# Cross attention of a two-layer model: keys turned by DMA, normalisation ahead of the reciprocal, routing of the last three groups in closer steps

## What is computed

```python
def _L1_xattn_ref(image_embeds, latents, ...):   # image_embeds = ctx, latents = layernorm(x)
    x = layer_norm(image_embeds, ln1_g, ln1_b)
    l = layer_norm(latents, ln2_g, ln2_b)
    q = l @ Wq                                    # 16 heads of 64
    kv = jnp.concatenate([x, l], axis=1) @ Wkv    # 64 + 64 rows a sequence
    ...                                           # softmax(q k^T / 8) v, then @ Wo
x = x + _L0_xattn_ref(...)
x = x + _L0_ffn_ref(...)
x = x + _L1_xattn_ref(ctx_1024, _layernorm(x), ...)
x = x + _L1_ffn_ref(_layernorm(x), ...)           # 8 experts, the best 2 of each token
```

## Time and profile before

| | |
|---|---|
| median of 3 runs | 1599.52 us (1598.59 to 1602.85) |
| the profiled execution | 1598.53 us |
| its span, first to last instruction | 1596.6 us |
| PE, busy time and share of the span | 1392.2 us, 87% |
| DVE | 1355.3 us, 85% |
| ACT | 1280.3 us, 80% |
| POOL | 1079.0 us, 68% |
| cross attention and routing | from some 395 us to 1311 us of the span |

### The profile page before, as it was taken

The page is one execution under the profiler, slowest core; times in us unless marked ns, Lnnn a source line. Parts: engine busy times, 40 slices in busy tenths (PEclk is TensorE's granted clock), DMA queues, the critical chain, the costliest instruction groups (busy, mean ns, idle before and its releaser), DMA issues. The chain is left out here.

```text
span 1596.6 us, 53031 instructions
## 1 busy us (share of the span) xinstructions
PE 1392.2 (87%) x17084; PEld 1186.1 (74%) x17084; DVE 1355.3 (85%) x3979; ACT 1280.3 (80%) x3930; POOL 1079.0 (68%) x1524
## 2 busy tenths in 40 slices
PE   4779889974799999999999999999999719999970
PEld 3667777763688888888888888888888618888860
DVE  4479999995799999999999999999999628888877
ACT  1358888875799999999999999999999616666645
POOL 0367877763666577887788778877887555666650
PEclk7989999986899999999999999999999959999995
DMA  5445553400100000000000000000000013332209
GB/s 145 140 158 180 192 202 148 160 2 5 27 13 12 13 20 20 23 22 19 18 22 22 18 18 22 22 18 18 22 15 9 22 43 91 87 84 77 80 28 316
DMA packets 99738, 101.83 MB, mean 64 GB/s; under 512 B 15305, under 2 KB 81132, under 8 KB 99457
## 3 DMA queue, kind: packets, MB, share of 16 engines
q1 hardware_dynamic: 82496, 78.77, 15.4%
q0 software_dynamic: 8640, 16.93, 3.2%
q10 hardware_dynamic: 8448, 4.20, 0.9%
HBM read 39.40 MB, written 57.16 MB: 60 GB/s over the span
## 5 line engine op out<-in xcount | busy, mean ns | idle before, releaser
L1227 ACT ACTIVATE c_p<-bank,c_nmax 128x128 f32<-128x128 f32 x1024 | 368.9, 401 | 2.2 <-DVE c_nmax L1081 1.3
L1016 POOL TENSOR_TENSOR c_p<-c_p,c_rden 128x512 f32<-128x512 f32 x256 | 266.8, 1042 | 110.4 <-DVE c_rden L1091 106.0
L1227 ACT ACTIVATION_READ_ACCUMULATOR c_p<-bank,c_nmax 128x1 f32 x1024 | 244.2, 241 | 0.0
L1403 POOL DMA_INDIRECT moe_outputs<-e_y,e_to x142 | 152.9, 1077 | 93.3 <-DVE e_y L1434 58.6
L112 PE MATMUL bank<-c_kvT,qk_fused 128*128 128x128 f16 x1024 | 185.8, 220 | 10.8 <-ACT c_kvT L1206 10.4
L1081 DVE TENSOR_REDUCE c_nmax<-bank 128x4 f32<-128x512 f32 x256 | 173.4, 677 | 17.5 <-PE bank L114 14.3
L114 PE MATMUL bank<-c_kvT,qk_fused 128*128 128x128 f16 x1024 | 185.7, 220 | 0.0
L113 PE MATMUL bank<-c_kvT,qk_fused 128*128 128x128 f16 x1024 | 185.7, 220 | 0.0
L1473 ACT ACTIVATE e_h<-bank,moe_b 128x256 f32<-128x256 f32 x284 | 117.9, 466 | 65.7 <-PE bank L114 64.4
L1297 PE MATMUL bank<-const,c_p 128*128 128x128 f32 x1024 | 155.9, 275 | 3.6 <-DVE c_pT0rest L1102 1.7
L1059 POOL DMA_INDIRECT moe_slots<-r_rows,r_pos x128 | 131.6, 1028 | 34.9 <-issue 34.9
(11 more groups left out here) (324 smaller groups left out, 5921.0 us busy)
## 6 DMA issues: line engine op xcount, KB each, us to landing
moe_slots<-slot_fill SPq DMA_DIRECT2D x66, 520.0 KB, 5.6
e_rows<-moe_slots SPq DMA_DIRECT2D x71, 130.0 KB, 2.2
f_z<-moe_outputs SPq DMA_DIRECT2D x32, 256.0 KB, 4.9
x<-in_x SPq DMA_DIRECT2D x16, 256.0 KB, 3.2
a_ctx<-in_ctx SPq DMA_DIRECT2D x32, 128.0 KB, 3.4
moe_stage<-in_L_ffn_W SPq DMA_DIRECT2D x16, 256.0 KB, 3.1
c_rows<-in_ctx SPq DMA_DIRECT2D x128, 32.0 KB, 2.0
c_rows<-x SPq DMA_DIRECT2D x128, 32.0 KB, 1.8
```

Of the source, the lines that this page charges most:

```text
L1016: pool.tensor_tensor(pr[r % 4][:], pr[r % 4][:], rep(rden[r % 4][:], 2, P), ALU.mult).then_inc(m["pn"], 1)
L1227: last = act.activation(pr[r % 4][:, h, :], SB[r % 2][:, P * h:P * h + P], ACT.Exp, bias=nmax[r % 4][:, h:h + 1], accum_out=den[r % 4][:, ...
L1403: pool.indirect_dma_start(s.z, bass.IndirectOffsetOnAxis(ap=to[t % YBUF][:, h:h + 1], axis=0), ys[t % YBUF][:, h, :], None, bounds_check=2 ...
```

## The change

- Keys: SP turns a tile's four f16 blocks with one transposing DMA, from `kvs` to `kvt`, which now has four buffers and a semaphore for each; TensorE's four transposes, ACT's copy and the waits that kept them apart from routing's use of the bank KVR go. G waits for the DMA. The row loads are made for two tiles at a time, four DMAs of 64 KB, two buffers.
- DVE: the normalisation of a tile's rows (`AT_KVN`) stands behind the row maximum and ahead of the reciprocal; before it stood at the end of the step, behind the statistics.
- Routing: the offsets of groups 0 to 12 are four steps smaller. Groups 13 to 15 have offsets of their own, with one step between an item and the next, and each of them has its own `rows`, `pf`, `pos` and scatter semaphore, so nothing waits for the landing of the scatters of the group before. The walk ends at step 282, not 299.

```diff
-        kvt = [sb(f"c_kvT{n}", [P, 2, 4, 64], F16) for n in range(2)]
+        kvt = [sb(f"c_kvT{n}", [P, 2, 4, 64], F16) for n in range(4)]
-        rows = sb("r_rows", [P, GT, ROW], F16)
+        rows = [sb(f"r_rows{n}", [P, GT, ROW], F16) for n in range(4)]
...
-        ROUTE_STATS = 14
-        ROUTE_RSTD, ROUTE_XN, ROUTE_XT, ROUTE_LOGITS, ROUTE_TOP, ROUTE_INDEX, ROUTE_MASK = 27, 32, 34, 38, 39, 42, 43
-        ROUTE_HIGH, ROUTE_LOW, ROUTE_STEP, ROUTE_BASE, ROUTE_POS = 44, 47, 45, 46, 47
+        EVEN = GROUPS - 3
+        ROUTE_STATS = 10
+        ROUTE_RSTD, ROUTE_XN, ROUTE_XT, ROUTE_LOGITS = (23, 23, 23), (28, 28, 24), (30, 29, 25), (34, 30, 26)
+        ROUTE_TOP, ROUTE_INDEX, ROUTE_MASK = (35, 31, 27), (38, 32, 28), (39, 32, 28)
+        ROUTE_HIGH, ROUTE_LOW, ROUTE_STEP = (40, 29, 25), (43, 30, 26), (41, 33, 29)
+        ROUTE_BASE, ROUTE_POS = (42, 33, 29), (43, 34, 30)
-        ROUTE_SCATTER = (48, 50, 51, 52, 54, 55, 56, 58)
-        FIRST, LO, HI, LAST = -15, 64, 240, CHUNKS + 43
+        ROUTE_SCATTER = tuple(zip((44, 46, 47, 48, 50, 51, 52, 54), (39, 40, 42, 43, 44, 46, 47, 48), (33, 34, 35, 36, 38, 39, 40, 41)))
+        FIRST, LO, HI, LAST = -15, 64, 224, CHUNKS + 26
...
+            if known(i):
+                for g in range(GROUPS):
+                    if 16 * i + k == 16 * g + at[min(max(g - EVEN + 1, 0), 2)]:
+                        return g
                 return None
+            return None if (k - at[0]) % 16 else i + (k - at[0]) // 16
+
+        def own(g):
+            return max(g - EVEN + 1, 0) if known(g) else 0
...
+            def load(n):
+                if n >= 2:
+                    sp.wait_ge(m["kvn"], 2 * n - 2)
+                for half in range(2):
+                    rows = slice(64 * half, 64 * half + 64)
+                    to = cs[n % 2]
+                    sp.dma_start(to[rows, :, 1 - half, :], cvw[1 - half, 2 * n:2 * n + 2, :, :].rearrange("t s d -> s t d")).then_inc(c_loaded[n % 2], 16)
+                    sp.dma_start(to[rows, :, half, :], s.xg(n // 2)[rows, 2 * (n % 2):2 * (n % 2) + 2, :]).then_inc(c_loaded[n % 2], 16)
+
+            def turn_keys(v):
+                sp.wait_ge(m["kv"], v + 1)
+                if v >= 4:
+                    sp.wait_ge(m["s"], 4 * (v - 3))
+                sp.dma_start_transpose(kvt[v % 4][:].rearrange("p n a c -> p (n a c)").rearrange("p (b c) -> p b c", b=4),
+                                       kvs[v % 4][:].rearrange("p n b d -> p (n b d)")).then_inc(kvt_in[v % 4], 16)
+
+            load(0)
+            load(1)
+            for v in range(TILES):
+                turn_keys(v)
+                if v % 2 == 1 and v + 3 < TILES:
+                    load((v + 3) // 2)
...
+                if t := tile(i, k, AT_KVN):
+                    v, r, g = t
+                    a, b = mv[r % 2], rst[r % 2]
+                    dve.wait_ge(m["rstd"], v + 1)
+                    wait(dve, m["kv"], v - 3)
+                    for n in range(2):
+                        last = dve.tensor_scalar(kv[r][:, n, :], cs[r // 2][:, r % 2, n, :], a[:, n, 0:1], b[:, n:n + 1], ALU.subtract, ALU.mult)
+                    last.then_inc(m["kvn"], 1)
...
-                if t := tile(i, k, AT_KVT):
-                    v, r, _ = t
-                    act.wait_ge(m["kvt"], v + 1)
-                    wait(act, m["s"], 4 * (v - 1))
-                    act.activation(kvt[r % 2][:].rearrange("p n a c -> p (n a c)"), KVB[:, 0:512], ACT.Copy).then_inc(m["kvt_copied"], 1)
...
                 if (g := group(i, k, ROUTE_HIGH)) is not None:
-                    wait(act, scattered, 128 * g)
-                    act.activation(rows[:, :, 0:D], r_xn[:], ACT.Copy).then_inc(mr["row_high"], 1)
+                    if own(g) == 0:
+                        wait(act, scattered[0], 128 * g)
+                    act.activation(rows[own(g)][:, :, 0:D], r_xn[:], ACT.Copy).then_inc(mr["row_high"], 1)
...
-                if t := tile(i, k, AT_KVT):
-                    pe.wait_ge(m["kv"], v + 1)
-                    wait(pe, m["kvt_copied"], v)
-                    for part in range(2):
-                        for b in range(2):
-                            at = 2 * P * part + P * b
-                            last = pe.transpose(KVB[:, at:at + P], kvs[r][:, part, b, :], s.ident_h[:])
-                    last.then_inc(m["kvt"], 1)
                 if n := number(i, k, AT_G, CHUNKS):
-                    if r % 4 == 0:
-                        pe.wait_ge(m["kvt_copied"], 4 * i + (k + AT_G) // 4 + 1)
+                    if u := tile(i, k, AT_G):
+                        pe.wait_ge(kvt_in[u[1]], 16 * (u[2] + 1))
```

More of the change, by code:

```diff
@@ L903, in cross_attention @@
     sem = s.sem
-    c_loaded = [sem(f"c_ctx_loaded{n}") for n in range(4)]
-    names = ("stats rstd kvn kv kvt kvt_copied g g_high g_copied s max exp rden pn pt pt_high pt_copied o o_high o_copied w x3")
+    c_loaded = [sem(f"c_ctx_loaded{n}") for n in range(2)]
+    kvt_in = [sem(f"c_kvt_in{n}") for n in range(4)]
+    names = ("stats rstd kvn kv g g_high g_copied s max exp rden pn pt pt_high pt_copied o o_high o_copied w x3")
     m = {n: sem("c_" + n) for n in names.split()}
@@ L908, in cross_attention @@
     mr = {n: sem("r_" + n) for n in route_names.split()}
-    scattered = sem("r_scattered")
+    scattered = [sem(f"r_scattered{n}") for n in range(4)]
     CHUNKS = 4 * TILES
@@ L944, in cross_attention @@
         pk = sb("r_pick", [P, 2, GT, EXPERTS])
-        pf = sb("r_posf", [P, 2, GT])
-        pos = sb("r_pos", [P, 2, GT], U32)
+        pf = [sb(f"r_posf{n}", [P, 2, GT]) for n in range(4)]
+        pos = [sb(f"r_pos{n}", [P, 2, GT], U32) for n in range(4)]
         zero = sb("r_zero", [P, 2, GT])
@@ L955, in cross_attention @@
         tx = sb("r_tx", [P, 72])
-        dest, first_choice = (rows[:, :, 2 * D + at:2 * D + at + 2].bitcast(F32) for at in (0, 2))
+        dest, first_choice = ([part[:, :, 2 * D + at:2 * D + at + 2].bitcast(F32) for part in rows] for at in (0, 2))
         block = ctx.enter_context(nc.Block())
@@ L959, in cross_attention @@
         PT, OB, KVR, WB = s.pb[4:8]
-        KVB = KVR[:].bitcast(F16)
         LOGITS = RANKS = KVR[:, 0:GT * EXPERTS]
@@ L999, in _ @@
         def _(sp):
-            def step(i, k):
-                t = 4 * i + k
-                if not (known(i) and i == 0):
-                    sp.wait_ge(m["kvn"], t - 3)
+            def load(n):
+                if n >= 2:
+                    sp.wait_ge(m["kvn"], 2 * n - 2)
                 for half in range(2):
                     rows = slice(64 * half, 64 * half + 64)
-                    sp.dma_start(cs[k][rows, 1 - half, :], cvw[1 - half, t, :, :]).then_inc(c_loaded[k], 16)
-                    sp.dma_start(cs[k][rows, half, :], s.xg(i)[rows, k, :]).then_inc(c_loaded[k], 16)
-            walk(sp, 0, TILES, 4, 4, TILES, step)
+                    to = cs[n % 2]
[13 more added lines that the diff above has]
+                    load((v + 3) // 2)
         @block.gpsimd
@@ L1068, in _ @@
             walk(pool, FIRST, LAST, 16, LO, HI, step)
-            pool.wait_ge(scattered, 128 * GROUPS)
+            pool.wait_ge(scattered[0], 128 * EVEN)
+            for q in range(1, 4):
+                pool.wait_ge(scattered[q], 128)
         @block.vector
@@ L1116, in step @@
                     dve.bn_aggr(mv[r % 2][:, 1, :], bst[:, 1, :]).then_inc(m["stats"], 1)
-                if t := tile(i, k, AT_KVN):
-                    v, r, g = t
-                    a, b = mv[r % 2], rst[r % 2]
-                    dve.wait_ge(m["rstd"], v + 1)
-                    wait(dve, m["kv"], v - 3)
-                    for n in range(2):
-                        last = dve.tensor_scalar(kv[r][:, n, :], cs[r][:, n, :], a[:, n, 0:1], b[:, n:n + 1], ALU.subtract, ALU.mult)
-                    last.then_inc(m["kvn"], 1)
                 if t := tile(i, k, -ROUTE_STATS):
                     v, r, g = t
+                    if not tile(i, k - 1, AT_STATS):
+                        dve.drain()
                     dve.bn_stats(r_bn[:, r, :], s.xg(g)[:, r, :])
@@ L1283, in step @@
                     v, r = n
-                    half, b, t = r % 2, r // 2 % 2, r // 4 % 2
+                    half, b, t = r % 2, r // 2 % 2, r // 4
                     pe.wait_ge(m["g_copied"], v + 2 if r % 4 == 0 else v - r % 4 + 4)
@@ L1288, in step @@
                         at = 8 * half + 2 * h
-                        last = parts_product(pe, SB[r % 2][:, P * h:P * h + P], [part[:, b, at:at + 2, :] for part in gs[t]],
+                        last = parts_product(pe, SB[r % 2][:, P * h:P * h + P], [part[:, b, at:at + 2, :] for part in gs[t % 2]],
                                              [kvt[t][:, part, 2 * b:2 * b + 2, :] for part in range(2)])
@@ L1316, in step @@
                     pe.wait_ge(mr["xn"], g + 1)
-                    wait_rows(i, k)
-                    wait(pe, mr["base_read"], g - 1 if ROUTE_XT + 16 < ROUTE_POS else g)
```

(1 more changed line is left out.)

52 lines of the change are left out of this document (21 added, 31 removed).

## The result

The changed kernel took 1595.45 us (median of 10 runs, 1590.74 to 1597.03) against 1600.38 us (10 runs) of the kernel before on the same chip: ratio 0.9969, 95% interval 0.9957 to 0.998. It is 5 us faster, and not 27.5: the time is 4 us above the upper end of the range, 1591 us, which is also that of rival (a). The profiled execution took 1595.94 us for a span of 1594.1 us.

The account below looks back on a forecast made before the run. The prediction took TensorE to bound the attention. Keys 28.1, start -3.5, order -9.1 and tail +12.0 made 27.5 us less: 1599.5 - 27.5 = 1572 us (forecast 1562 to 1580, chance 0.52; range 1553 to 1591).

Parts of the forecast that it names:

- rival (a): Attention: engines behind TensorE swallow the keys' gain, attention gains 0 to 10 us, time 1581 to 1591 us; chance 0.23.
- ACT was what was late there: Attention: TensorE's wait for ACT's copy of the turned keys goes without a next wait replacing it; 14.0 us kept.
- the 14.1 us of the turns: Attention: removing four key turns from TensorE saves 0.22 us a tile over 64 tiles, 14.1 us.
- the two terms: Attention: key turns off TensorE, 14.1 us, and the wait for the keys' copy gone, 14.0 us; sum 28.1 us.
- The term of the copy: Attention: waits for ACT's copy of the turned keys, 10.4 + 4.6 = 15.0 us, of which 14.0 us counted as gain.
- the bound of the stretch without routing: Attention's 16 chunks without routing: TensorE never waits and its work, 50.6 us, makes up the 50.5 us measured.
- Keys, forecast 24.6 us less with the start: Attention: keys by DMA gain 28.1 us, less 3.5 us at the start.
- Start, forecast 3.5: First tile: nothing covers the turned transfer before the first G product; cost 3.5 us, bounds 1 and 7.
- Transfer, forecast 4 us and hidden: Each tile's turned 128 KB DMA: 2.6 to 6.2 us, taken as 4, hidden inside about 7 us in steady state.
- Order, forecast a loss of 9.1: DVE's normalisation ahead of the reciprocal delays p rest: loss of 0.7 us in each of 13 groups, 9.1 us.
- Tail, forecast 12.0: Routing behind the attention: the last group's first scatter starts at 1285.5, 12.0 us sooner than 1297.57; bounds 10 and 13.

Follow-up runs that it names:

- e18: The kernel before with the keys' transfer alone (normalisation at the end of VectorE's step, rstd at offset 13, routing as before): 1602.75 us, ratio 1.0014.
- e17: The kernel before, unchanged, as a control: 1600.7 us, ratio 1.0001.
- e3: The kernel before with only the normalisation moved ahead of the reciprocal; keys turned by TensorE, routing as before: 1601.3 us, ratio 1.0006.
- e4: The changed kernel with the routing's offsets of before and one row buffer for every group: 1596.91 us, ratio 0.9976.
- e2: The changed kernel with GpSimd's rstd of the keys' rows one step sooner (offset 14, not 13): 1586.91 us, ratio 0.9917.
- e13: The changed kernel with rstd at offset 14 and the rest part of the heads' outputs for one head of eight only: 1642.59 us, ratio 0.9839.
- e9: The kernel before with the normalisation ahead of the reciprocal and rstd at offset 14; keys turned by TensorE, routing as before: 1696.62 us, ratio 1.0109.
- e15: The changed kernel with rstd at offset 14, same as e2, repeated as a control on another chip: 1668.18 us, ratio 0.9973.
- e10: The changed kernel with rstd at offset 14 and the routing's offsets and single row buffer of before: 1675.43 us, ratio 1.0003.
- e1: The changed kernel with the normalisation of the keys' rows behind the statistics again, at the end of VectorE's step: 1597.58 us, ratio 0.9979.

## Why the prediction was wrong

**Which step failed.** "ACT was what was late there, and it gets to its next copy, of p, about half a microsecond sooner than now, so I keep all: 14.0 us", and with it the 14.1 us of the turns. TensorE did run into the next wait. With the keys' transfer alone (e18 against e17, on one chip) the two terms, 28.1 us by the forecast less 3.5 for the start, brought nothing: 1602.75 against 1600.7 us, and a pace 0.34 us a group higher. That the turns went is seen chunk by chunk. The table shows, for each step of a group, the time from the start of TensorE's turn of p to the start of the next one (medians of nine groups, us, from the starts of those matmuls):

```
step              0    1    2    3    4    5    6    7    8    9   10   11   12   13   14   15    sum
before (e17)   3.32 3.93 3.58 3.10 3.32 3.10 3.96 3.10 3.32 3.10 3.10 3.18 3.47 3.28 3.44 3.25  53.57
order (e3)     3.63 3.63 3.58 3.10 3.52 3.25 3.96 3.10 3.32 3.10 3.10 3.10 3.50 3.25 3.23 3.10  53.47
keys (e18)     3.10 3.66 3.69 3.10 3.10 3.52 4.04 3.10 3.10 3.10 3.17 3.63 3.25 3.75 3.44 3.25  54.01
keys+order(e4) 3.62 3.25 3.58 3.10 3.76 3.25 3.96 3.10 3.10 3.10 3.10 3.14 3.73 3.25 3.23 3.10  53.36
after          3.61 3.25 3.96 3.10 3.10 3.18 3.10 3.18 3.83 3.25 3.23 3.10 3.73 3.25 3.54 3.10  53.54
rstd 14 (e2)   3.10 3.25 3.96 3.10 3.10 3.10 3.10 3.22 4.05 3.25 3.22 3.10 3.91 3.25 3.55 3.10  53.37
```

From before to keys alone each of steps 0, 4, 8 and 12 loses 0.22 us, the turns, 0.88 us in all, as forecast. Step 1 loses another 0.27: of the 0.66 us that TensorE waited there for the copy, the rest is lost to the next wait in the same step, now for the rest of G. Steps 5, 11 and 13 then give back 0.42, 0.45 and 0.47, steps 2 and 6 0.2: VectorE is now what is late. The term of the copy was also too large by its own rows: 10.4 + 4.6 us counts the six waits twice that stand under PE and under PEld alike. Each counted once, the 17 waits come to 11.9 us, 2.3 of them at the first three tiles.

That the bound has changed engine is seen by following the waits back from TensorE's matmul at 1100 us to 620 us, at each instruction to what released it, or else to the one before it on its engine (share of the 480 us):

```
                        PE   DVE   ACT  POOL
before (e17)            73    13    14     0
order alone (e3)        79     5    14     2
keys alone (e18)        41    46    13     0
after                   17    52     0    31
rstd sooner (e2)        37    62     0     0
lighter VectorE (e13)   68    21    10     0
```

The shares say which engine holds the chain, not how long a group is: in e9, with a pace of 54.98, TensorE has 54 and VectorE 46. Even before, a quarter of the chain did not run through TensorE. The prediction took the bound of the stretch without routing, where TensorE never waits, for that of the middle, where VectorE has 4 us more work a group. In e2 the chain of each group is one piece of 32.9 us on VectorE, its instructions back to back, and one of 20.5 us on TensorE. The kernel lets TensorE run only one chunk ahead of p rest, since the turned p has one bank; that this is why neither engine fills the other's thin chunks is argued, not shown.

**Term by term.** Keys, forecast 24.6 us less with the start: alone +2 us (0 to 4, e18); on top of the new order -5 (e3 to e4), none of it in the pace; with rstd sooner -18 to -19 from the pace (e9 against e15 and e10), because e9 is slow and not because e10 is fast. Start, forecast 3.5: first load to first G product is 1.6 us longer. Transfer, forecast 4 us and hidden: 2.9 us from the start of the issue, which takes 1.2 of them, hidden in every tile but the first. (The landings in the rows include the issue too, so the 0.6 us that the prediction added for it was counted twice; it changes nothing.) The estimate from the Trainium skill ("VectorE: DVE Perf Modes", The three transpose paths), 1309 ns a block and so 5.2 us for four, was too dear here. The same page's preference for TensorE (Rules for kernel authors), which the prediction set aside, came out right for the keys' transfer alone.

Order, forecast a loss of 9.1: nothing alone (e3), and with the keys' transfer a gain of 6 us (e18 to e4, 1.0014 to 0.9976). The wait for rstd was foreseen and real (8.8 us in 400), but it hid the other half: at its old place the pair costs more, 0.64 us an instruction (e1) against 0.42. The Trainium skill ("SBUF — State Buffer", Who interferes with whom), with its lock between VectorE's fast modes and GpSimd, pointed the right way: by that rule alone the move would only gain, and the instructions of the pair did become shorter in e3 too (0.37 against 0.52 us in e17), though there the time didn't.

Tail, forecast 12.0: 10.3. POOL had more left than I counted: five of group 14's eight scatters stand before rstd and hold it up until 2.3 us behind the statistics, three more stand behind it. What I had not priced is that the same scatters, laid closer under groups 13 to 15, slow these: 5.2 us in groups 14 and 15, and 7 us in the whole stretch, against e4. Net the routing gave 1 us in the changed kernel and 5.6 us with the pair at its old place (e18 to e1).

Rival (a) named the mechanism, its price was too low: it kept tail and start as net 8.5 us, and took the attention never to be slower than before; by the two traces its stage is 3.8 us longer.

**What stays open.** Why rstd sooner, worth 8 us with the keys' transfer, costs about 1 us a group without it (pace 53.56 in e3, 54.98 in e9, of which 0.4 is the chip); steps 0, 11 and 12 grow from 3.63, 3.10 and 3.50 to 3.89, 3.81 and 4.06. A part of step 12 is `r_eq`, 0.19 us in e3 and 0.58 in e9, where it meets the multiplication of p; the rest has no cause. How much faster the kernels with rstd sooner would be with `r_eq` elsewhere. Why the same kernel's pace differs between chips by 0.4 us: between e2 and e15 it is all in steps 0 and 7, and the durations of DVE's and POOL's instructions agree, but for a pair that is shorter in e15 (0.34 us an instruction against 0.37). What the loads of two tiles at a time did, which came with the keys' transfer in every run; no wait of VectorE for `c_rows` shows behind the first tiles. And whether a second bank for the turned p would bring the rest: all eight banks are taken, and it wasn't tried.

## To carry to other kernels

When several engines are each within 5% of the pace, taking work from the one that looks full may buy nothing, as here by itself, and it can cost: follow the chain of waits through the stretch in question and see what share of it the engine holds before pricing a removal. Test a bundle of edits as a table of combinations, since here the keys' transfer was worth -2, +5 or +18 us according to where two VectorE instructions and three small GpSimd ones stood; and compare each cell with the kernel before too, since the +18 was measured from a combination that had itself become slower. Look up in the trace how much time an edit really took from the engine before it counts as a test: cutting two instructions from 128 to 4 columns took 0.13 us, not 0.6. And work moved under the last chunks of a loop isn't free because the engine has idle time; look at who waits for its small instructions there.

## What the hardware showed beyond that

A drain on GpSimd soon behind a scatter held the next instruction up. In the changed kernel 0.14 us lie between the first and the second instruction of rstd where no scatter had ended in the 3 us before, and 0.26 to 1.89 us in the 37 tiles where one had (0.25 to 0.64 in the kernel before). Over 600:1000 the waits come to 14.7 us in the changed kernel and 7.0 in the kernel before; with rstd a step sooner (e2) all are 0.14 us.

```profile
POOL c_rstd L1046 <- issue: 14.7, 22, 1.3
```

```profile
POOL c_rstd L1024 <- issue: 7.0, 22, 0.6
```

VectorE's TENSOR_TENSOR `r_eq` of 128x32 values, 0.19 us where it begins outside GpSimd's multiplication of p, took 0.58, 1.05 or 1.78 us where the multiplication ran or began beside it, and ended 0.06 us after it each time (e2, e13, e14).

A turned transfer of 128 KB within SBUF took 1.20 us of its queue's time against 0.61 us for a row load of 64 KB, and landed 2.4 to 3.9 us after the start of its issue beside other traffic. Two of the chips took 18 to 29% longer for the same stage of scatters, gathers and weights behind the attention, and at most 1.3% longer for the attention itself (873.1 against 862.0 us in the sooner-rstd kernel).
